# Integer inputs in two loaded halves, six kept groups of up products, and a joint product and maximum

## The reference

```
x = act_qdq(layernorm(x1))                 # act_qdq: scale = max|.|/32767 over the WHOLE tensor,
up   = act_qdq(x @ w_up.T)                 #          round to that grid, times scale
gate = act_qdq(x @ w_gate.T)
sig  = round(sigmoid(gate)*65536)/65536
gate = act_qdq(gate * sig)
o    = act_qdq(gate * up)
out  = x1 + tanh(g_ffn) * (o @ w_down.T)
```

## Time and profile before

| | us |
|---|---|
| median of the runs | 1842.2 |
| profiled execution, its own time | 1842.63 |
| its span | 1840.6 |
| gate stage, first product to its barrier | 1237.6 to 1387.2 |
| up stage | 1395.0 to 1557.4 |
| hidden stage with its scale chain | 1557.4 to 1687.4 |
| down stage | 1687.4 to 1840.6 |

### The profile page before, as it was taken

How to read it: one execution, slowest core, us unless ns; L and a number is a source line. 1 busy time by engine, 2 the same in 40 slices (tenths; PEclk the granted TensorE clock), 3 DMA queues, 4 the chain that set the end, 5 groups by cost and what they waited for, 6 DMA issues and landing times. The chain is left out here.

```text
span 1840.6 us, 36804 instructions
## 1 busy us (share of the span) xinstructions
PE 1722.7 (94%) x12200; PEld 1452.0 (79%) x12200; DVE 1375.7 (75%) x2260; ACT 1128.3 (61%) x3073; POOL 427.1 (23%) x373
## 2 busy tenths in 40 slices
PE   6899999999999999999999999959997887997998
PEld 5788888888888888888888887848885665786998
DVE  6667667677676676776766768758888998998785
ACT  4656566556566565565665655646656887664665
POOL 2222313323223232232232322210002332431000
PEclk9999999999999999999999999989998998998999
DMA  5010001000010011010100010016774563334664
GB/s 183 13 37 25 23 24 44 26 24 34 28 32 23 24 35 34 24 34 20 40 23 24 34 36 12 24 64 231 261 253 151 182 185 99 129 135 153 210 202 148
DMA packets 58600, 151.14 MB, mean 82 GB/s; under 512 B 4416, under 2 KB 33728, under 8 KB 56640
## 3 DMA queue, kind: packets, MB, share of 16 engines
q1 hardware_dynamic: 58560, 150.62, 24.3%
HBM read 85.07 MB, written 65.54 MB: 82 GB/s over the span
## 5 line engine op out<-in xcount | busy, mean ns | idle before, releaser
L320 POOL TENSOR_TENSOR prob<-prob,rsums 128x512 f32<-128x512 f32 x256 | 261.1, 1040 | 755.3 <-DVE rsums L497 755.3
L357 ACT ACTIVATE prob<-masked,neg_max 128x128 f32<-128x128 f32 x1024 | 396.0, 391 | 7.2 <-DVE neg_max L463 3.8
L368 ACT ACTIVATE qT<-proj 128x512 f32<-128x512 f32 x128 | 76.6, 598 | 260.9 <-PE proj L606 260.9
L479 DVE COPY probT<-trans 128x512 f32<-128x512 f32 x128 | 88.3, 690 | 152.6 <-PE trans L641 148.8
L357 ACT ACTIVATION_READ_ACCUMULATOR prob<-masked,neg_max 128x1 f32 x1024 | 195.6, 191 | 0.0
L463 DVE TENSOR_REDUCE neg_max<-masked 128x4 f32<-128x512 f32 x256 | 175.7, 686 | 8.8
L461 DVE TENSOR_TENSOR masked<-score,mask_add 128x512 f32<-128x512 f32 x256 | 174.1, 680 | 1.4 <-PE score L666 0.6
L758 PE MATMUL pair<-xThi,wup_hi 128*128 128x512 f32 x360 | 144.7, 402 | 28.4 <-POOL xTlo L1232 16.9
L641 PE MATMUL trans<-ident,prob 128*128 128x128 f32 x1024 | 153.3, 272 | 1.6 <-ACT probT L377 1.6
L677 PE MATMUL y<-wo_hi,o_hi 128*128 128x256 f32 x512 | 147.3, 288 | 3.6 <-DVE o_lo L503 3.6
L485 DVE COPY v_sb<-proj 128x512 f32<-128x512 f32 x128 | 88.5, 691 | 80.7 <-PE proj L606 80.0
(11 more groups left out here) (190 smaller groups left out, 4503.6 us busy)
## 6 DMA issues: line engine op xcount, KB each, us to landing
gate<-gate_d SPq DMA_DIRECT2D x30, 768.0 KB, 4.2
gate_d<-stage SPq DMA_DIRECT2D x8, 1536.0 KB, 6.0
n_u_d<-w_raw SPq DMA_DIRECT2D x16, 768.0 KB, 3.6
stage<-n_u_d SPq DMA_DIRECT2D x16, 768.0 KB, 5.9
gate_d<-gate SPq DMA_DIRECT2D x7, 1536.0 KB, 6.0
x_in<-in_x SPq DMA_DIRECT2D x16, 512.0 KB, 3.9
ctx_in<-in_ctx SPq DMA_DIRECT2D x16, 512.0 KB, 3.6
x_d<-x SPq DMA_DIRECT2D x16, 512.0 KB, 4.5
```

Source lines behind the costliest of these rows:

```text
L320: gp.tensor_tensor(pr, pr, rsums[:, h, :].rearrange("p (b o) -> p b o", o=1).broadcast_to([P, NB, P]), ALU.mult).then_inc(normed, 1)
L357: nc.scalar.activation(prob[:, c % 2, h, b, :], masked[:, h, b, :], ACT.Exp, bias=neg_max[:, h, b:b + 1], accum_out=psums[:, h, b:b + 1]). ...
L479: nc.vector.tensor_copy(probT[:, 1], trans[:]).then_inc(probT_copied[1], 1)
```

## The change

In the gate stage ScalarE rounds x into one tile `n_full`; VectorE makes two integer tiles from it, the upper bits (`& -16`) and the lowest four (`& 15`), and both are stored (the stored `n_x` doubles to 512 KB per group). The matmuls' `hi` and `lo` parts are then plain copies of the two by ScalarE, in every stage; GpSimd does nothing after the attention stage, and `x_wide` is gone.

In the up stage PSUM holds four pairs in a ring instead of three. Groups 0, 4, 8, 12 and the last two are kept: after VectorE's maximum, ScalarE copies the pair to `stage` in the step of the next group (`keep`), and SyncE stores the group of 1.5 MB to `up_d` (not for the last two, which stay). In the hidden stage six groups are read back and ten are multiplied again, in the order kept, again, again, kept, ...; the loads are issued ahead. `n_u` has three buffers instead of two. In the third part of the kept groups and of every second recomputed one (11 groups), ScalarE writes magnitudes of `n_p` and of the rounded up values as 16-bit integers (`magnitude`), and VectorE takes product and maximum in one instruction (`largest_product`). The stage is straight-line code. The down stage's first loads are issued after all stores of `n_u` have landed. The core of the diff:

```diff
+            def quantise_x(t):
+
+                wait(act, x_split, 2 * t)
                 for k in range(KC):
                     act.wait_ge(x_transposed, KC * t + k + 1)
-                    nc.scalar.activation(n_x[:, b, k, :], tr[k][:], ACT.Copy, scale=inv_x[:, 0:1]).then_inc(x_int, 1)
+                    nc.scalar.activation(n_full[:, k, :], tr[k][:], ACT.Copy, scale=inv_x[:, 0:1]).then_inc(x_int, 1)
+                act.wait_ge(x_split, 2 * t + part + 1)
+                nc.scalar.activation(xT[b][part][:], n_x[:, b, part], ACT.Copy).then_inc(x_ready, 1)
...
+            def split_x(t, b):
+
+                dve.wait_ge(x_int, KC * (t + 1))
+                wait(dve, n_x_stored[b], 8 * (t - b))
+                wait(dve, x_ready, 2 * (t - 1))
+                v.tensor_scalar(n_x[:, b, 0], n_full[:], -LOW, None, ALU.bitwise_and).then_inc(x_split, 1)
+                v.tensor_scalar(n_x[:, b, 1], n_full[:], LOW - 1, None, ALU.bitwise_and).then_inc(x_split, 1)
...
-            def step(t, b, more):
-                if more:
-                    wait(sp, x_high, KC * t)
+            def store_up(t, q):
+                sp.wait_ge(staged, PAIRS * (q + 1))
+                sp.dma_start(up_d[:, bass.ds(q, 1)].rearrange("p o n -> p (o n)"), stage[0][:]).then_inc(up_stored, 16)
...
-            def high(t, b):
+            def widen(t, b):
                 act.wait_ge(x_loaded[b], 8 * t + 8 * b)
-                wait(act, x_ready, KC * (t - 1))
-                nc.scalar.activation(x_wide[:], n_x[:, 1 - b], ACT.Copy).then_inc(x_widened, 1)
                 wait(act, product_done, PAIRS * (t - 1))
-                for k in range(KC):
-                    nc.scalar.activation(xT[1 - b][0][:, k, :], n_x[:, 1 - b, k, :], ACT.Copy).then_inc(x_high, 1)
+                for part in range(2):
+                    nc.scalar.activation(xT[1 - b][part][:], n_x[:, 1 - b, part], ACT.Copy).then_inc(x_ready, 1)
...
+            def keep(t, r, q, i):
+
+                if not kept(t, r):
+                    return
+                act.wait_ge(reduced, PAIRS * t + i + 1)
+                if r == 0 or t == G - 2:
+                    wait(act, up_stored, 16 * q if r == 0 else 16 * (G // 4))
+                to = stage[1 if isinstance(t, int) and t == G - 1 else 0]
+                nc.scalar.activation(to[:, i * PN:(i + 1) * PN], pair[((r * PAIRS + i) % RING)][:], ACT.Copy).then_inc(staged, 1)
+
+            def step(t, r, q):
+                first = isinstance(t, int) and t == 0
+                round_gate(t, 0)
+                if not first:
+                    keep(*before(t, r, q), 0)
+                sigmoid(t, 0)
+                round_gate(t, 1)
+                if not first:
+                    keep(*before(t, r, q), 1)
+                    keep(*before(t, r, q), 2)
+                sigmoid(t, 1)
+                if not (isinstance(t, int) and t == G - 1):
+                    widen(t + 1, 1 - r % 2)
+
+            by_fours(act, G, step)
+            act.wait_ge(ahead.loaded[0], 16)
+            act.wait_ge(product_done, PAIRS * (G - 1))
+            for part in range(2):
+                nc.scalar.activation(xT[1][part][:], n_x[:, 1, part], ACT.Copy).then_inc(ahead.ready, 1)
+            for i in range(PAIRS):
+                keep(G - 1, 3, G // 4 - 1, i)
...
+                pe.wait_ge(reduced, n - RING + 1)
+                at = before(*before(t, r, q)) if i == 0 else before(t, r, q)
+                if kept(*at[:2]):
+                    pe.wait_ge(staged, staged_before(at[0], at[2]) + (i - 1) % PAIRS + 1)
...
+    BUFS = 3
+    kept = [G - 2, G - 1] + list(range(0, G, 4))
+    again = [t for t in range(G) if t not in kept]
+    order = []
+    for n in range(len(kept)):
+        order += [("kept", n)] + [("again", m) for m in range(2 * n, 2 * n + 2) if m < len(again)]
+    order = order[:-1] if len(order) > G else order
+    order = [o for o in order if o != ("again", len(again) - 1)] + [("again", len(again) - 1)]
...
+    def by_magnitude(p):
+
+        return order[p][0] == "kept" or order[p][1] % 2 == 1
...
+            def widen(m):
+
+                act.wait_ge(ahead.loaded[m % 2], 16 * (m // 2 + 1))
+                act.wait_ge(product_done, PAIRS * (m - 1))
+                for part in range(2):
+                    nc.scalar.activation(xT[(m + 1) % 2][part][:], n_x[:, (m + 1) % 2, part], ACT.Copy).then_inc(x_ready, 1)
...
+            def magnitude(p, part, source):
+
+                n = magnitudes(p)
+                wait(act, hid_reduced, PAIRS * (by_place[n - 2] + 1) if n >= 2 else 0)
+                nc.scalar.activation(p_abs[:, n % 2], n_p[:, step_of(p), part], ACT.Abs).then_inc(magnitude_done, 1)
+                nc.scalar.activation(u_abs[:, n % 2], source, ACT.Abs, scale=k_u[:, 0:1]).then_inc(magnitude_done, 1)
+
+            act.wait_ge(scale_step, 4)
+            for p, (kind, n) in enumerate(order):
+                wait(act, stored[p % BUFS], 16 * (p // BUFS))
                 for i in range(PAIRS):
+                    wait(act, hid_reduced, PAIRS * (p - BUFS) + i + 1)
                     part = slice(i * PN, (i + 1) * PN)
-                    if on_chip(t):
-                        source = up[b][:, part]
+                    if kind == "kept":
+                        wait(act, up_loaded[n % 2], 16 * (n // 2))
+                        source = up[n % 2][:, part]
                     else:
-                        act.wait_ge(product_done, PAIRS * (t - 2) + i + 1)
-                        source = pair[i][:]
-                    nc.scalar.activation(n_u[:, b, part], source, ACT.Copy, scale=k_u[:, 0:1]).then_inc(up_int, 1)
-                if not (isinstance(t, int) and (t == 0 or t >= G - 2)):
-                    high(t + 2, b)
-
-            act.wait_ge(scale_step, 4)
-            two_buffers(act, G, step)
+                        act.wait_ge(product_done, PAIRS * n + i + 1)
+                        source = pair[(PAIRS * n + i) % RING][:]
+                    if i == PAIRS - 1 and by_magnitude(p):
+                        magnitude(p, part, source)
+                    nc.scalar.activation(n_u[:, p % BUFS, part], source, ACT.Copy, scale=k_u[:, 0:1]).then_inc(up_int, 1)
+                if p == 0:
+                    widen(1)
+                elif kind == "again" and n + 2 < len(again):
+                    widen(n + 2)
...
+            def largest_product(p, i):
+
+                n, m = PAIRS * p + i, magnitudes(p)
+                wait(dve, hid_reduced, n - PAIRS + 1)
+                dve.wait_ge(magnitude_done, 2 * (m + 1))
+                v.tensor_tensor_reduce(hid[:, part(i)], p_abs[:, m % 2], u_abs[:, m % 2], 1.0, 0.0, ALU.mult, ALU.max,
+                                       amax_hid[:, n:n + 1]).then_inc(hid_reduced, 1)
...
-                largest(PAIRS - 1)
-
-            two_buffers(dve, G, step)
+            for p in range(G):
+                times(p, 0)
+                times(p, 1)
+                largest(p, 0)
+                if by_magnitude(p):
+                    largest(p, 1)
+                    largest_product(p, 2)
+                else:
+                    times(p, 2)
```

More of the change, by code:

```diff
@@ L1134, with up_pair @@
 PAIRS = 3
[L1137 removed]
+RING = 4
+def up_pair(nc, pair, wup, xT, i):
     KC, T = wup[0].shape[1], NB * P
[L1140 to L1146 removed]
+    for e in range(2):
+        n = 2 * i + e
+        last = product(nc, pair[:, e * T:(e + 1) * T], lambda s, k: wup[s][:, k, n * P:(n + 1) * P],
+                       lambda m, k: xT[m][:, k, :], KC)
+    return last
 class Ahead:
@@ L1214, in _ @@
+            def step(t, r, q):
+                b = r % 2
+                if not last_two(t):
+                    wait(sp, x_ready, 2 * t)
+                    load_x(t + 2, b)
+                if not (isinstance(t, int) and t == G - 1):
+                    for h in range(2):
+                        sp.wait_ge(rounded[h], t + 1)
+                        load_gate(t + 1, h)
+                if r == 1:
+                    store_up(t - 1, q)
             load_x(1, 1)
-            with sp.Fori(0, G // 2 - 1) as i:
-                for b in range(2):
-                    step(2 * i + b, b, True)
@@ L1327, in hidden_max, with step, step_of, magnitudes @@
+            def step(t, r, q):
+                wait(pe, x_ready, 2 * t)
+                for i in range(PAIRS):
+                    read_before(t, r, q, i)
+                    up_pair(nc, pair[(r * PAIRS + i) % RING], wup, xT[1 - r % 2], i).then_inc(product_done, 1)
+            by_fours(pe, G, step)
+def hidden_max(nc, ident, ones, n_x_d, n_u_d, up_d, wup, n_x, xT, up, n_u, hid, n_p, ahead, prefetch, amax_up, amax_hid, s_x, s_p, s_hid, G, N):
     KC, T = wup[0].shape[1], NB * P
     PN = 2 * T
-    x_loaded, x_widened, x_high, x_ready = ahead.loaded, ahead.widened, ahead.high, ahead.ready
+    BUFS = 3
[6 more added lines that the diff above has]
+    order = [o for o in order if o != ("again", len(again) - 1)] + [("again", len(again) - 1)]
```

(49 more changed lines are left out.)

265 lines of the change are left out of this document (92 added, 173 removed).

## The result

The changed kernel took 1810.2 us (median of four runs, 1809.13 to 1811.13) against 1841.55 for the kernel before (now four runs), a ratio of 0.9825 (95% interval 0.9811 to 0.9838). Forecast were 1808.0, within 1801 to 1819. The profiled execution took 1809.69 us, its span is 1807.9. The gain is 31.4 us by the medians and 32.7 by the two spans; the terms of the forecast add up to 34.4.

The account below looks back on a forecast made before the run. TensorE was taken to bound the gate and hidden stages, VectorE the up stage. 1842.6 + 0.6 - 12.2 - 22.8 = 1808.2, about 1808 us; range 1801 to 1819, leaving about two in ten out.

Parts of the forecast that it names:

- Gate stage, +0.6: Gate stage: TensorE still bounds it; only the first group's longer chain to TensorE's start shows, +0.6 us.
- Up stage, -12.2: Up stage: GpSimd gone -11.2, last two groups' waits -3.2, last pair's copy +1.1, ScalarE after group 0 +1.1: -12.2 us.
- Hidden stage, -22.8: Hidden stage: with 30 TensorE pairs instead of 42, VectorE is last; 107.2 us against 130.0, -22.8 us.
- The joint term: Hidden stage: one joint product and maximum with its accumulator read costs VectorE 1.41 us (1.22 + 0.19), in 11 groups.
- The waits of VectorE: Hidden stage: VectorE waits 1.1 us for the first copy and 4 for the second kept group's first copy.
- Down stage, 0: Down stage: keeps its instructions, so no change in time; 153 us expected.
- The dear joint instruction: Rival, hidden stage: the joint instruction costs as much as the two it replaces, 2.4 us; kernel 1817; chance 0.14.
- Loads that bind the up stage: Rival, up stage: gate halves land in 7.5 us instead of 4.2, four stalls of 2 us; kernel 1817; chance 0.06.
- a slow multiplication that stays: Rival, up stage: something other than GpSimd lengthens the multiplication, so the -11.2 us goes; kernel 1819; chance 0.04.
- It does better: Rival, hidden stage: joint instruction at its floor (1.22 us) and no early wait; kernel 1802; chance 0.09.
- The slow clock: Rival: TensorE at its lower level (1.2 GHz) through the hidden stage, 51 us longer; kernel 1859; chance 0.03.
- the prediction's sign of a granted clock under 0.9: Sign that the prediction is wrong: TensorE's granted clock under 0.9 outside the stages' edges.

Follow-up runs that it names:

- thirteen with the late loads: Changed kernel with earlier input loads, second kept group right behind the first, joint instruction in thirteen groups, down-stage loads still after the last store: 1801.75 us, 0.9776.
- the first two runs with two kept: Changed kernel with only the last two groups kept, fourteen recomputed: with the joint instruction 1828.31 us (0.9922), without it 1825.98 us (0.9911).
- the run with GpSimd busy again: Changed kernel plus two unused 128x512 f32 subtractions by GpSimd in each of fourteen up-stage groups: 1824.54 us, 0.9907.
- two kept, plain: Changed kernel with only the last two groups kept, fourteen recomputed, and no joint instruction: 1825.98 us, 0.9911.

## Why the prediction was right, and where it was off

*Gate stage, +0.6.* Measured +0.9, and that it came so near is luck. TensorE's first product waits 1.55 us for ScalarE after and 0.93 before; this is the term of the forecast, +0.5 by the start of that product.

```profile
1236.92 0.50 PE L747 MATMUL ring<-xThi,wgate_hi 128*128 128x512 f32 x1 [1.55 <-ACT xTlo L856]
```

But in the 4 us from there TensorE's granted clock is 0.57, against 1.00 before, and its next transposes start 9.9 us behind the first product instead of 8.3: +1.6, which the forecast did not have. A wait of 1.54 us for a load of `xin` in the execution before is 0.30 in this one, -1.2. The low clock is no fixed price: in the twelve profiled executions with this gate stage the wait is 1.5 to 1.6 us in all, yet six open at 0.57 and take 161.1 to 162.2 us, and six open at 1.00 and take 159.9 to 160.8. What decides between them no run shows. The doubled store was free.

*Up stage, -12.2.* Measured -12.4, and the term that carries it is shown: idle work on GpSimd brings the slow multiplications back. The last two groups' 3.2 us are gone, and the copies behind the last maximum hold the end for 1.36 us instead of 0.32, the forecast's +1.1. ScalarE after group 0 costs VectorE one wait of 0.81 us (forecast 1.1). Gate halves land in 5.2 us, under the 7.3 allowed, so the loads never bound it.

*Hidden stage, -22.8.* The mechanism held: VectorE last, 98.5 of 109.8 us busy, TensorE 88.2. Two sizes of the sum were off, in opposite directions. The joint term: start to start the instruction and its read take 1.14 to 1.22 us, not 1.41, some 2.6 us over eleven groups to the good; the forecast had taken the length of a product's row (1.22) as its base, where a product costs 1.14 from start to start, and ScalarE's dear read on top. The waits of VectorE: 1.1 + 4 in the forecast, 9.5 measured. I had counted the start only and written of the moved loads that they would be hidden; I looked at the four for the down stage and not at the inputs' load, which the order puts behind the store of its group and, once in three groups, behind a 1.5 MB load: the one shown is issued 8.5 us after its buffer is free and lands 8.8 us later. It costs ScalarE 5.6 us in three waits and the stage 3.8 (109.4 to 105.6). -2.6 + 4.4 is 1.8 of the 2.2 us missing; that the two errors partly cancel is luck. The moved loads at the end were hidden as forecast (0.3 us to the barrier). Without that lead the gap was 5.39 us for the 6 named, but only 2.0 of them came from the loads; 3.35 stayed with the loads long issued, for the late last store.

*Down stage, 0.* Measured +0.7. In its first 20 us TensorE's granted clock was 0.66, and 0.69 before; over the executions of all versions that share went from 0.62 to 0.73, and the stage from 152.5 to 155.4 us. Two things can be told apart there: where the short load comes 1.6 us or more behind the mask (thirteen with the late loads, and the first two runs with two kept) the stage takes 154.7 or more; the remaining 1.5 us of spread goes roughly with the clock of that stretch, from 152.55 us at 0.73 to 154.07 at 0.66. That the clock is its cause isn't shown, since no experiment set it.

*The rivals.* The dear joint instruction fell by its row. Loads that bind the up stage and a slow multiplication that stays fell by the traces above. *It does better* had the joint instruction right and the early waits wrong; its 1802 was reached only with the loads and the order changed (1801.69). The slow clock did not come: the hidden stage as a whole has 0.90, low in its first 6 us, as before, and at its end, where TensorE has nothing to do, and once between. But the prediction's pauses of TensorE were too short: 0.9 us in the up stage measured up to 1.40 (clock 1.00 there), and "under 1 us" in the hidden stage measured 2.73, 1.49 and 2.74, each a wait for ScalarE to empty a pair's buffer. Behind the first of them, and so inside the stage, the prediction's sign of a granted clock under 0.9 did appear:

```profile
1590.00:1600.00 10.00, 7.27 (x26) 5.50 (x25) 9.28 (x10) 10.00 (x11) 0.00 (x0) 0.83 0.50 164
1570.00:1580.00 10.00, 9.73 (x44) 7.72 (x43) 8.62 (x9) 10.00 (x11) 0.00 (x0) 1.00 0.71 229
1630.00:1640.00 10.00, 7.26 (x33) 5.68 (x32) 10.00 (x10) 10.00 (x11) 0.00 (x0) 1.00 0.38 157
```

With a pause of 0.27 the ten microseconds have 1.00, with the one of 2.73 they have 0.83, and with the one of 2.74 again 1.00. So the clock sank for some 3 us behind one pause and not behind another just as long; the pause alone does not tell when, and TensorE had the time to spare. The Trainium skill (TensorE: Matmul & The Clock Gate, "A second HAM failure mode: psum-queue depth-cycling") warns of swings for short idles from PSUM cycling; single drops of this kind show here, but no repeated swinging in any stage.

## What to carry to other kernels

The parts of a change are not a sum: with TensorE last the joint instruction shortened nothing (the hidden stage grew by 3.3 us), with VectorE last it took 4.1 us from the stage, and a ScalarE fed in time made room for the next step. When work moves to an engine beside the last one, follow that engine's own inputs, each load with what stands ahead of it in the issuing queue, as closely as the last engine's instructions. And before an engine's work is called free because it is off the path, look at which instructions of the last engine grow while it runs.

## What the runs showed of the hardware

In these rows GpSimd and VectorE do not share, they take turns, in VectorE's rounding and in its multiplication but not in its maximum. With GpSimd's two subtractions issued together (the run with GpSimd busy again), GpSimd and VectorE of the up stage:

```profile
1460.19 3.26 POOL L1313 TENSOR_TENSOR stage<-stage 128x512 f32<-128x512 f32 x2 [4.29 <-ACT xTlo L1257]
```

```profile
1459.77 1.22 DVE L1333 TENSOR_REDUCE ext_gate<-pair 128x1024 f32 x1
1460.90 1.40 DVE L1326 TENSOR_SCALAR w_raw<-w_raw 128x1536 uint16<-128x1536 f32 x1
1462.45 2.62 DVE L1328 SCALAR_TENSOR_TENSOR n_p<-n_g,k_p,w_raw 128x1536 int16 x1
```

Undisturbed, two subtractions took 1.28 us each in the mean in the kernel before (from 1549.62 us, VectorE idle beside the first, at a maximum beside the second):

```profile
L1238 POOL TENSOR_TENSOR xTlo<-w_raw,xThi 128x512 fp32r<-128x512 f32 x2 | 2.5, 1281 | 8.3 <-ACT xThi L1272 8.3
```

If the first runs alone, until 1461.5, the rounding (0.95 alone), which starts at 1460.90, should end some 0.6 late; it ends 0.45 late. The second subtraction then starts near the rounding's end, at 1462.2, and ends at 1463.45; the multiplication (1.82 alone), which starts at 1462.45, should be late by 1.0 and is late by 0.8. The maximum at 1459.77, from PSUM, keeps its 1.22, and so does the one of the kernel before that ran beside the second undisturbed subtraction and read `stage`, a tile in SBUF:

```profile
1550.93 1.22 DVE L1300 TENSOR_REDUCE ext_gate<-stage 128x1 f32<-128x1024 f32 x1 [1.95 <-ACT stage L1276]
```

So it is not SBUF alone that decides.

The Trainium skill (SBUF — State Buffer, "SBUF: two separate sides") says that the port pair of the two engines is locked for a whole instruction of GpSimd, or of VectorE with two SBUF inputs or in a two-port mode, and that the other blocks. These rows agree to 0.2 us, and the maximum in SBUF, with its one input, does not speak against it. The multiplication has two SBUF inputs; the rounding has one, and whether it ran in a two-port mode the rows don't say. The same working fits the slow multiplication of the earlier trace rows: the second subtraction, behind a rounding that ends at 1442.57, would end 1.28 us later, at 1443.8, and the pair ended at 1443.70.

The joint product and maximum over 1024 columns of 16 bits takes as long as the product alone (1216 against 1219 ns), and its read 82 ns, where ScalarE's read of an accumulator takes 191.

A load of 0.5 KB issued behind four of 512 to 768 KB on the same queue lands 5.2 us (changed kernel) to 6.7 us later (two kept, plain), and 2.5 where they are gone before it.
